# A fused decoder layer on one core: the attended context written already turned, with the softmax scaled before its turn instead of after

## The reference, cut to what matters

```
cq = jnp.einsum('bcd,bqd,d->bcq', c, q, w_cq) + b_cq
s = (c @ w_c + b_c)[:, :, None] + (q @ w_q + b_q)[:, None, :] + cq
a = jax.nn.softmax(s, axis=2)
c2q_att = jnp.einsum('bcq,bqd->bcd', a, q)
b_att = jax.nn.softmax(jnp.max(s, axis=2), axis=1)
q2c_att = jnp.einsum('bc,bcd->bd', b_att, c)[:, None, :]
x = jnp.concatenate([c, c2q_att, c * c2q_att, c * q2c_att], axis=-1)
z = x @ W_l.T + b_l
```

## Time and profile before

| | |
|---|---|
| median of three executions | 685.49 us |
| the profiled execution | 685.69 us |
| its span | 683.9 us |
| TensorE busy | 659.3 us (96%), 3880 matmuls |
| VectorE busy | 476.2 us (70%) |
| ScalarE busy | 359.2 us (53%) |
| GpSimd busy | 251.5 us (37%) |

### The profile page before, as it was taken

How to read it: one execution, slowest core, us unless ns; L and a number is a source line. 1 busy time by engine, 2 the same in 40 slices (tenths; PEclk the granted TensorE clock), 3 DMA queues, 4 the chain that set the end, 5 groups by cost and what they waited for, 6 DMA issues and landing times. The chain is left out here.

```text
span 683.9 us, 11790 instructions
## 1 busy us (share of the span) xinstructions
PE 659.3 (96%) x3880; PEld 561.6 (82%) x3880; DVE 476.2 (70%) x1236; ACT 359.2 (53%) x826; POOL 251.5 (37%) x322
## 2 busy tenths in 40 slices
PE   3999999999999999999999989999999999999997
PEld 1778978888789788887886878888888888888886
DVE  4587777777776777777878977765667657577433
ACT  3656766667566766675686344442423334233321
POOL 2136356173452651734552522332333232322231
PEclk9999999999999999999999999999999999999999
DMA  7615134043151340431633180323213132220300
GB/s 210 162 27 161 48 90 143 3 117 116 32 166 35 91 142 0 129 105 42 183 113 90 32 261 28 125 93 125 92 26 130 61 124 92 106 81 2 140 15 32
DMA packets 51774, 64.44 MB, mean 94 GB/s; under 512 B 3912, under 2 KB 49528, under 8 KB 50848
## 3 DMA queue, kind: packets, MB, share of 16 engines
q1 hardware_dynamic: 51744, 64.06, 30.6%
HBM read 56.60 MB, written 7.45 MB: 94 GB/s over the span
## 5 line engine op out<-in xcount | busy, mean ns | idle before, releaser
L1600 POOL TENSOR_TENSOR xt<-xt,cw_wide 128x512 f32<-128x512 f32 x55 | 72.1, 1311 | 176.9 <-ACT xt L1558 176.9
L1624 DVE TENSOR_TENSOR res<-bank,xt 128x512 f32<-128x512 f32 x61 | 41.9, 687 | 57.8 <-POOL xt L1600 53.4
L1562 ACT ACTIVATE a_hi<-res 128x512 fp32r<-128x512 f32 x42 | 26.6, 634 | 99.1 <-DVE res L1624 99.1
L75 PE MATMUL bank<-h_hi,w_lo 128*128 128x512 f32 x168 | 67.8, 404 | 1.6 <-DVE w_lo L1641 0.8
L76 PE MATMUL bank<-h_lo,w_hi 128*128 128x512 f32 x168 | 66.3, 395 | 0.0
L77 PE MATMUL bank<-h_hi,w_hi 128*128 128x512 f32 x168 | 66.3, 394 | 0.0
L75 PE MATMUL bank<-w_hi,op_lo 128*128 128x256 f32 x184 | 53.3, 290 | 0.6 <-DVE w_lo L1217 0.6
L76 PE MATMUL bank<-w_lo,op_hi 128*128 128x256 f32 x184 | 51.6, 281 | 0.0
L77 PE MATMUL bank<-w_hi,op_hi 128*128 128x256 f32 x184 | 51.5, 280 | 0.0
L1016 POOL TENSOR_TENSOR wz_lo<-tmp,wz_hi 128x512 fp32r<-128x512 f32 x28 | 37.0, 1330 | 34.1 <-ACT wz_hi L781 33.8
L1629 DVE TENSOR_TENSOR a_lo<-res,a_hi 128x512 fp32r<-128x512 f32 x42 | 33.6, 800 | 22.4 <-ACT a_hi L1562 22.4
(11 more groups left out here) (248 smaller groups left out, 2083.6 us busy)
## 6 DMA issues: line engine op xcount, KB each, us to landing
cw_wide<-in_ctx_t SPq DMA_DIRECT2D x32, 375.0 KB
ctxf<-in_ctx SPq DMA_DIRECT2D x32, 375.0 KB
cw_wide<-cw_scratch SPq DMA_DIRECT2D x7, 1536.0 KB, 7.8
xt<-in_x SPq DMA_DIRECT2D x8, 448.0 KB, 4.0
x_scratch<-x2b SPq DMA_DIRECT2D x8, 448.0 KB, 3.2
x2n<-x_scratch SPq DMA_DIRECT2D x7, 512.0 KB, 4.7
cw_wide<-cw_scratch SPq DMA_DIRECT2D x7, 512.0 KB, 4.4
x2t<-x_scratch SPq DMA_DIRECT2D x7, 512.0 KB, 4.0
```

Of the source, the lines that this page charges most:

```text
L75: pe.matmul(dst, a_lo, b_hi, start=first, stop=False, **kw)
L1562: act.activation(a_hi[n % (AHEAD + 1)][:, :], af[(p + n) % 2][:, :], ACT.Copy).then_inc(a_hi_ok, 1)
L1600: pool.tensor_tensor(sg[b][:, :], sg[b][:, :], cw_wide[p][:, ORDER[n], :], ALU.mult).then_inc(sgw_ok, 1)
L1624: dve.tensor_tensor(af[b][:, :], u_bank[b][:, :], sg[b][:, :], ALU.mult).then_inc(af_ok, 1)
```

## The change

`c2q_product` swaps its operands: the context becomes the weights, in two column halves of 128, and `at` (112 columns) moves. The result comes out as 128 by 112, twice, which is what `turn_x` made before, so `turn_x` and `c2q_copy` are gone. Since the division by the row's sum can no longer be done after the product (the rows now lie along the free side), VectorE does it before the first turn, in place on `tmp[j]`: the new `scale_a`, a reciprocal of the stream's own sum and a product over 375 columns. `turn_a` waits for it. In the queues, `x_high` moves to the places of the copies, the transposes of `m4` on TensorE go behind the third product, and `normalise_h` on VectorE goes ahead of `mneg`.

```diff
                     def turn_a(j):
-                        pe.wait_ge(exp2_ok, ev[j])
+                        pe.wait_ge(a_ok, ev[j])
...
                     def c2q_product(j):
                         pe.wait_ge(at_ok, ev[j])
-                        for b in range(NSB):
-                            last = pe.matmul(bank[j][0:L, 0:D], at[j][:, b * L:(b + 1) * L], ctxf[0:SB, j, b, :], start=(b == 0),
-                                             stop=(b == NSB - 1))
+                        for k in range(KB):
+                            for b in range(NSB):
+                                last = pe.matmul(bank[j][:, k * L:(k + 1) * L], ctxf[0:SB, j, b, k * P:(k + 1) * P],
+                                                 at[j][:, b * L:(b + 1) * L], start=(b == 0), stop=(b == NSB - 1))
                         last.then_inc(c2q_mm, 1)
-
-                    def turn_x(j):
-                        pe.wait_ge(c2q_ok, ev[j])
-                        for k in range(KB):
-                            last = pe.transpose(bank[j][:, k * L:(k + 1) * L], tmp[j][0:L, k * P:(k + 1) * P], ident[0:L, 0:L])
-                        last.then_inc(t_x, 1)
...
-                    def c2q_copy(j):
-                        act.wait_ge(c2q_mm, ev[j])
-                        act.wait_ge(sinv2_ok, ev[j])
-                        act.activation(tmp[j][0:L, 0:D], bank[j][0:L, 0:D], ACT.Copy, scale=sinv2[:, j:j + 1]).then_inc(c2q_ok, 1)
-
-                    def x_high(j):
-                        act.wait_ge(t_x, ev[j])
+                    def x_high(j):
+                        act.wait_ge(c2q_mm, ev[j])
...
+                    def scale_a(j):
+                        dve.wait_ge(exp2_ok, ev[j])
+                        dve.reciprocal(sinv2[:, j:j + 1], ssum2[:, j:j + 1]).then_inc(sinv2_ok, 1)
+                        dve.wait_ge(sinv2_ok, ev[j])
+                        dve.tensor_scalar(tmp[j][0:L, 0:S], tmp[j][0:L, 0:S], sinv2[:, j:j + 1], None, ALU.mult).then_inc(a_ok, 1)
...
                     sim_max(1)
+                    scale_a(0)
                     c_weighted(3)
...
-                    dve.wait_ge(exp2_ok, ev[G - 1])
-                    dve.reciprocal(sinv2[:, :], ssum2[:, :]).then_inc(sinv2_ok, G)
                     if last:
                         route_groups(dve, 0)
+                    if not last:
+                        normalise_h(i + 1)
                     dve.wait_ge(t_m, i + 1)
```

More of the change, by code:

```diff
@@ L390, in decoder_layer @@
             t_a, at_ok = sem("a_transposed"), sem("a_columns_ready")
-            c2q_mm, c2q_ok = sem("c2q_product"), sem("c2q_copied")
-            t_x, x_hi_ok, x_lo_ok = sem("c2q_transposed"), sem("c2q_hi_ready"), sem("c2q_lo_ready")
+            a_ok, c2q_mm = sem("a_scaled"), sem("c2q_product")
+            x_hi_ok, x_lo_ok = sem("c2q_hi_ready"), sem("c2q_lo_ready")
             x3_ok, x3_hi_ok, x3_lo_ok = sem("c_c2q_ready"), sem("c_c2q_hi_ready"), sem("c_c2q_lo_ready")
@@ L718, in group @@
                         pe.wait_ge(h3_lo_ok, KB)
+                    c2q_product(2)
                     pe.wait_ge(m4_ok, G * (i + 1))
                     pe.transpose(m_bank[0:G, 0:L], m4[:, :], ident[0:L, 0:L]).then_inc(t_m, 1)
-                    c2q_product(2)
-                    turn_x(0)
                     c2q_product(3)
-                    turn_x(1)
                     if not last_group:
@@ L727, in group @@
                     z_c2q(0)
-                    turn_x(2)
-                    turn_x(3)
                     z_c2q(1)
@@ L933, in group @@
                     c_high()
+                    x_high(0)
                     a_columns(3)
[L935 to L938, removed]
+                    x_high(1)
+                    x_high(2)
                     act.wait_ge(mneg_ok, i + 1)
                     act.activation(mexp[:, :], m_bank[0:G, 0:L], ACT.Exp, bias=mneg[:, :], accum_out=msum[:, :]).then_inc(mexp_ok, 1)
-                    x_high(1)
-                    c2q_copy(3)
+                    x_high(3)
                     if not last:
@@ L945, in group @@
                     x3_high(0)
-                    x_high(2)
                     x3_high(1)
-                    x_high(3)
                     x3_high(2)
@@ L1282, in group @@
                     sim_max(2)
+                    scale_a(1)
                     if not is_first(i):
@@ L1285, in group @@
                     row_term(0)
+                    sim_max(3)
+                    scale_a(2)
                     row_term(1)
-                    sim_max(3)
                     row_term(2)
+                    scale_a(3)
                     row_term(3)
@@ L1301, in group @@
                         normalise3(dve, 1)
-                    else:
-                        normalise_h(i + 1)
                     x_low(0)
```

## The result

The changed kernel takes 686.69 us (median of 20 executions, 685.55 to 689.83), the kernel before, run beside it, 685.71 us (20 executions, 684.28 to 687.22). The ratio is 1.0021 with a 95% interval of 1.0011 to 1.0031: slower by 1.4 us, between 0.8 and 2.1. The forecast was 691.6, slower by 6. The direction was right; the size was wrong by a factor of about four, and the time lies where the rival "about the same" had it. Three executions over 1.5% above the fastest of their kernel (733, 733 and 1318 us) are left out of the medians and ratios of the experiments.

A forecast was written before the change was run, and what follows sets the result against it. TensorE bounds the middle groups, but VectorE's full queue makes its turns wait. From 685.69 us, middle groups add 2.8, first 1.2, last 2.1: 691.8, or 691.6 against the median; 8-in-10 range 685.5 to 698.

The forecast's parts named there:

- about the same: Rival: shorter steps and records at 0.095 us; middle groups gain a little, first and last lose 3; 685 to 687, chance 0.08.
- the chain of VectorE to the third turn: Middle group: VectorE's queued work up to the third scale_a ends at 232.41, so TensorE's third turn waits 0.57 us.
- The handover to TensorE: Each wait of TensorE on VectorE: 0.23 us from VectorE's end to the turn's start, possibly 0.1 off.
- the three turns' waits: Middle group: TensorE waits for scaled exponentials before the first three turns, part of 1.09 us of waiting a group.
- the likeliest case: TensorE waits on VectorE's new steps, 1.09 us a middle group; 691.6 us, slower by 6, chance 0.70.
- break-even of a middle group: Middle group: TensorE's own work falls by about 0.6 us, so waiting above 0.6 makes the group longer.
- The first group: Four statistics delay the second turn by 1.84 us; after 0.39 back from saved transposes, the group loses 1.2 us.
- The last group: VectorE works without a gap until the first x_low, so its new work lands on the end: 2.1 us.
- The product: TensorE's swapped product: twelve records at 0.112 us, 1.34 us a stream, with 1.14 as the low end.
- The new product on VectorE: The tensor_scalar over 375 columns in scale_a: 0.41 us, between bounds of 353 and 458 ns.
- The lock: Rival: GpSimd's small steps lock VectorE out of SBUF beside scale_a, 10 us over seven groups; 701 us, chance 0.10.
- `normalise_h` "costs nothing": Middle group: normalise_h ahead of mneg ends near 236.0; mrow is ready about 238.2, before its use at about 239.3.

The follow-up runs named there:

- the mended one: Changed kernel with the last group the old way, scale_a steps earlier and three first-group statistics moved into VectorE's waits, against the kernel before: 682.13 us, ratio 0.9949.

## Why the prediction was wrong

**The step that failed** is the chain of VectorE to the third turn, "from 230.12 to 232.41. The third turn starts at 232.64 (231.52). Here TensorE waits longest, 0.57 us". The mechanism was right, the queue's order and every instruction in it too; the durations in it were too long by 0.57 us in 5.35:

- Each `sim_max` was counted with 0.55, its time from start to end. Its successor starts 0.44 to 0.47 behind its start (226.95 to 227.42, 228.78 to 229.22, 230.68 to 231.14). Three of them: 0.28 less. The forecast subtracted this overlap from the new steps, which it took as 0.54 instead of 0.61, and not from `sim_max`; the earlier trace rows had it, 228.53 to 228.99.
- The `row_term` was counted with 0.53, the distance between two of them. Ahead of a `sim_max` it is 0.34 (230.34 to 230.68), and the same ahead of a reciprocal: the 0.19 belongs to a `row_term` behind a `row_term` (231.66 to 232.18 is 0.52 again) and not to its own time. The trace of the kernel before had this too: the `row_term` at 230.12 is followed 0.35 later by

```profile
230.47 0.54 DVE L1196 TENSOR_REDUCE smx<-bank 112x1 f32<-112x375 f32 x1
```

- The new step moves the queue on by 0.52 instead of 0.54, and the moments and `ctw` are 0.04 shorter: together about 0.1.
- The handover to TensorE, taken as 0.23, is at most 0.19 here: the product at 227.60 ends at 228.02 and its turn starts at 228.21. At the third turn it is 0.17: the product behind it starts at 232.21, 0.31 earlier is 231.90, and the new product on VectorE ends at 231.73.

So the three turns' waits of 0.13, 0.19 and 0.57 became 0, 0 and about 0.25; only similarity 3 kept its 0.20. The middle groups then lose 0.45 of waiting and gain 0.59 of work: -0.14 each, where +0.46 was forecast. This is 3.7 us, of the 4.7 between the forecast loss of 6.1 and the measured 1.4; at equal clock, with a loss of 2.5, it is all of the difference of 3.6. The run without `scale_a` and the mended one show the same 0.45 from both sides. The corrected durations were taken from the changed kernel's own trace and then put to three new orders and loads: they gave 45.0, 44.75 and 46.7 us a middle group, measured are 44.86, 44.76 and 46.77.

**Where the likeliest case was decided.** The forecast put the break-even of a middle group at 0.6 us of waiting, which the run without `scale_a` confirms (0.59). It had 1.09 and allowed 0.1 for each handover and 0.05 for a step, but nothing for the old instructions' durations, since these stood in rows. The doubt belonged there too: a term that is counted three times in a row has to be the distance between starts. The rival "about the same" had 0.08. Its time (685 to 687), its small gain in the middle groups and its 3 lost at the ends are near what happened, but not its cause: it asked for records at 0.095 together with shorter steps, and the records took 0.112 and a step 0.52 instead of 0.54. That its time came true is luck; nothing in the prediction named old instructions counted too long.

**The first group**: forecast +1.2, measured +0.8 to +1.5. The second turn, forecast at 1.84 late, waited 1.27 by the view and 1.53 by distances (from the similarity at 46.60 to the product at 49.71 there are 3.11 instead of 1.27 + 0.31). Moving the statistics away brought the group to 45.97 and the wait to 0.27.

**The last group**: forecast +2.1, measured +1.7 and returned by the run with the old last group. Right in kind: VectorE's work lands on the end. From the second `sim_max` to the first `x_low` VectorE takes 12.48 instead of 10.80 us: four steps of 0.52, less 0.09 for the old reciprocal, less 0.19 because one `row_term` fewer stands directly behind another, less 0.13 in which VectorE had stood idle behind the second `sim_max`. The last two terms were missing.

**The product**: twelve records at 0.112, 1.34, exactly as taken from the earlier trace rows; the low end of 0.095, by moving columns alone, is refuted. **The new product on VectorE**: forecast 0.41; all 32 of them:

```profile
L1184 DVE TENSOR_SCALAR tmp<-tmp,sinv x32: 414/416/423, 45.4 to 371.9; 112x375 f32<-112x375 f32 x32
```

**The lock.** Refuted by the same line: none of the 32 was longer than 423 ns. The one at 229.40 took 0.42 though it lies inside the first of the two GpSimd steps below, and a `row_term`, with two inputs in SBUF, took its usual 0.42 at 231.66, inside the second:

```profile
229.37 1.02 POOL L981 TENSOR_TENSOR ln<-ln,mhalf 112x4 f32<-112x4 f32 x1
...
231.45 1.16 POOL L985 TENSOR_TENSOR ln<-ln,mhalf 112x4 f32<-112x4 f32 x1
```

That an operation on 4 elements holds the port only briefly is still my reading, not shown. The rule weighed in the prediction (the Trainium skill, "SBUF — State Buffer", section "SBUF: two separate sides"), by which the holder keeps the shared pair for its whole instruction, agrees with `mrow`, which ends 0.07 behind `c_lo` here, and not with the two instructions beside L981 and L985.

**`normalise_h` "costs nothing"**: right, `mrow` is ready at 237.47 against its use at 238.55. But the sentence hid a dependence: the move is what makes room for the later turn of `m4`. Without it the group loses 0.91, more than the 0.59 that the smaller work on TensorE gains.

**The whole**: 0.8 to 1.5 for the first group, -0.9, and 1.7 give +1.6 to +2.2; two timings say 0.8 to 2.1 and 0.6 to 2.8, and 2.5 at equal clock. What lies between these is within the scatter of the stretches outside the groups.

## What to carry to other kernels

When a queue is summed to say when something is ready, count each instruction by the distance from its start to its successor's, with a neighbour of the same kind as in the new place; only the last link counts to its end, and a duration that stands three times in the chain carries its error three times. When work moves to an engine with spare time, the price is set by what stands ahead of it in the queue, not by its size alone: the same four steps cost a middle group 0.45 us in one order and nothing in another, and in the first order, made 0.45 longer each, another 1.57. Look apart at the first and last turn of a loop, where other work fills the very places that are free in the middle ones.

## What the runs showed of the hardware that was not expected

- TensorE's wait of about 0.25 us at the third turn isn't marked in the timeline: it shows in a row of 0.58 instead of 0.48 or 0.49 and in the distance between starts.
- A `row_term` (a product with a running sum) is followed by a `sim_max` or a reciprocal after 0.34 to 0.35 us, by another `row_term` after 0.52.
- `mrow`, 4 rows by 112, takes as long as GpSimd's `c_lo` still runs: 0.81 us in the changed kernel and 1.39 with `normalise_h` moved back, each time ending 0.07 behind it. Beside GpSimd's four `x2b` it is less regular: in the last group of both kernels an `x3_low` took 2.14 us, over several of them, while in the middle group those at 238.49 and 239.56 took 0.55 and 0.38 though `x2b` ran. What decides this is not shown.
- The kernel before took 1.2 to 1.8 us longer (medians, in two sets of timings) where its mean granted clock was 0.992 to 0.994 instead of 0.998 or more; in the traces the lower level stands behind the last group.
- Two profiles of the same kernel differ by 2.4 us in the startup before the first group while the six middle groups agree within 0.05, so a stretch is to be compared where it repeats.
